# Unit 0 normalised on VectorE and convolved head by head, one Toeplitz side for the first two units, first loads in a new order

## What is computed

```python
x = x + xattn(layernorm(x), k, bias, ctx, ctx, 8)        # v, k, bias, x1, x2
    kv  = v[:, h, i, None, :] * x2[:, h, None, j, :]      # 16 heads of 8 rows
    y   = causal_conv(kv, k[h]) + kv * bias               # 256 positions
    out = sum over i of y[h, i, j, :] * x1[h, i, :]
x = x + ffn(layernorm(x))                                 # 2048 tokens, 16 experts, top 4, and a shared one
```

## Time and profile before

| | |
|---|---|
| time, median of 3 runs | 398.09 us (397.99 to 398.44) |
| span of the profiled execution | 395.4 us |
| mean granted TensorE clock over the span | 0.998 |
| busy: TensorE, VectorE, ScalarE, GpSimd | 384.7, 244.1, 162.9, 180.3 us |

### The profile page before, as it was taken

One profiled execution on the slowest core, in us unless ns is written; L12 is line 12 of the kernel. 1 busy time (PEld: TensorE's weight loads), 2 busy tenths in 40 slices (PEclk: granted clock), 3 DMA queues, 4 the chain that ended last, 5 costly groups with the idle time before them and its releaser, 6 DMA issues.

```text
span 395.4 us, 9070 instructions
## 1 busy us (share of the span) xinstructions
PE 384.7 (97%) x2146; PEld 279.3 (71%) x2147; DVE 244.1 (62%) x676; ACT 162.9 (41%) x494; POOL 180.3 (46%) x225
## 2 busy tenths in 40 slices
PE   6999999999999999999999999999999999999996
PEld 6788888888888546555667675446767777777765
DVE  3577577987988465788735344443445464646466
ACT  5347656564564362101124333333333333334431
POOL 3254323337888573565553333333333333334333
PEclk9999999999999999999999999999999999999999
DMA  7974474368879996256376873334474737362737
GB/s 248 363 254 139 163 277 144 133 206 278 309 250 335 414 419 258 96 207 223 104 215 219 321 239 107 87 95 134 127 246 136 242 115 242 115 232 103 264 97 251
DMA packets 37812, 83.09 MB, mean 210 GB/s; under 512 B 5930, under 2 KB 25870, under 8 KB 35728
## 3 DMA queue, kind: packets, MB, share of 16 engines
q1 hardware_dynamic: 31248, 64.83, 49.1%
q0 software_dynamic: 6528, 17.84, 11.6%
HBM read 60.21 MB, written 23.48 MB: 212 GB/s over the span
## 4 chain that ended last, share of the span: by engine, by line
PE 79%; DVE 10%; DMA 4%; issue 2%; ACT 2%; SPq 1%; DVEq 1%; POOL 0%; POOLq 0%
PE heads L1382 18%; PE bank L1456 13%; PE heads L1271 11%; PE heads L1424 7%; PE heads L1273 5%; PE bank L1437 5%; PE heads L1392 4%; PE bank L1403 4%; PE bank L1285 3%; DVE kv L734 3%; PE heads L1374 3%; DMA toep<-toep_in 2%; PE bank L1448 2%; DVE prod L763 2%; DMA y_scratch<-toep,dest_i 2%
## 5 line engine op out<-in xcount | busy, mean ns | idle before, releaser
L716 POOL DMA_INDIRECT y_scratch<-toep,dest_i x72 | 71.8, 997 | 112.0 <-DVE dest_i L1131 96.0
L1382 PE MATMUL heads<-experts,toep 128*128 x256 | 86.6, 461 | 0.6 <-DVE toep L1089 0.5
L1271 PE MATMUL heads<-toep,kv 128*128 128x256 f32 x256 | 77.9, 386 | 1.9 <-DVE kv L734 0.8
L661 POOL DMA_INDIRECT rows_scratch<-rows,slot_i x64 | 63.3, 989 | 35.4 <-issue 19.5
L1456 PE MATMUL bank<-experts,toep 88*128 x256 | 66.2, 381 | 1.6 <-DVE toep L1096 1.6
L553 ACT ACTIVATE toep<-heads 128x176 f32<-128x176 f32 x72 | 22.8, 317 | 78.1 <-PE heads L1382 67.2
L1382 PEld LDWEIGHTS heads<-experts,toep 128*128 128x128 f32 x256 | 43.7, 190 | 14.8 <-issue 1.1
L1273 PEld LDWEIGHTS heads<-toep,kv 128*128 128x128 f32 x256 | 48.7, 190 | 6.5
L763 DVE TENSOR_TENSOR prod<-heads,ctx_rep 128x1024 f32<-128x1024 f32 x32 | 39.1, 1221 | 22.3 <-PE bank L1285 19.9
L1096 DVE COPY toep<-heads 88x256 f32<-88x256 f32 x72 | 30.2, 419 | 31.1 <-PE heads L1392 31.1
L1273 PE MATMUL heads<-toep,kv 128*128 128x128 f32 x256 | 49.2, 274 | 0.0
(11 more groups left out here) (240 smaller groups left out, 513.4 us busy)
## 6 DMA issues: line engine op xcount, KB each, us to landing
ctx_rep<-ctxr_in SPq DMA_DIRECT2D x16, 1024.0 KB, 5.0
experts<-experts_in SPq DMA_DIRECT2D x16, 608.0 KB
toep<-rows_scratch SPq DMA_DIRECT2D x56, 144.0 KB
prod<-y_scratch SPq DMA_DIRECT2D x5, 1024.0 KB, 5.5
rows_scratch<-pad_row SPq DMA_DIRECT2D x17, 144.0 KB, 1.8
ctx_tr<-ctxt_in SPq DMA_DIRECT2D x16, 128.0 KB
toep<-toep_in SPq DMA_DIRECT2D x4, 512.0 KB, 7.0
ctx_n<-ctx_in SPq DMA_DIRECT2D x16, 128.0 KB, 2.1
```

What stands on the lines that cost most here:

```text
L661: pool.indirect_dma_start(rows_d, bass.IndirectOffsetOnAxis(ap=slot_i[:, u, k:k + 1].bitcast(U32), axis=0), rows[:, u, :], None).then_inc( ...
L716: pool.indirect_dma_start(y_d, bass.IndirectOffsetOnAxis(ap=dest_i[b][:, 0:1].bitcast(U32), axis=0), y_sb[b], None, bounds_check=TOPK * TO ...
L1271: nc.tensor.matmul(y_ps[par][:, i, :], kv[:, q, 0, h * P:(h + 1) * P], toep[:, q * HH + h, :], start=True, stop=False)
L1382: last = nc.tensor.matmul(up_ps[p], x_tr[p][:, blk, :], up_w(e, blk), start=blk == 0, stop=blk == LB - 1)
```

## The change

Units 1 and 2 change places in the processing order (`ORDER`), so that the first two units both hold heads 0 to 7; `SIDE` tells each place's half of `toep` and of `skip_w`. The second Toeplitz half is loaded behind unit 1's context and unit 2's ctx_tr, and `convolve` waits for it at u = 2. Within `toep` and `ctx_rep` heads are stored even first, then odd; a half of `toep` is waited for by parity, and ctx_rep of units 0 and 1 comes in two transfers, one for each parity. x of unit 0 has a transfer and a semaphore of its own.

Unit 0 is normalised on VectorE (`first_v`, with the power still on GpSimd); ScalarE starts with unit 1. The even heads' outer product of unit 0 is made and signalled head by head (`kv_heads_even`), and `convolve(0, 0)` waits for each head. In unit 0 VectorE does `kv_blocks(1)` before both products, and TensorE does `skip_sum(0)` after `convolve(0, 1)`. `skip_w` is made on GpSimd, behind the bias, which is loaded later. There are 14 and 4 warm-up transposes instead of 22 and 10. The host permutes the inputs and puts the output back in order.

```diff
+ORDER = (0, 2, 1) + tuple(range(3, UNITS))
+SIDE = tuple(u % 2 for u in ORDER)
...
-WARM_UP = 22
-WARM_ON = 10
+WARM_UP = 14
+WARM_ON = 4
...
+            def load_rep_half(u, par):
+
+                half = HH // 2 * L
+                sp.dma_start(ctx_rep[:, u, par * HH // 2:(par + 1) * HH // 2, :].rearrange("p h l -> p (h l)"),
+                             ctxr_d[u][:, par * half:(par + 1) * half]).then_inc((rep_odd if par else cr_in)[u], 16)
...
-            load_x(0, 2, x_in[0])
+            load_x(0, 1, x_first)
+            load_x(1, 2, x_in[0])
+            load_tr(0)
+            load_toep(0, 0)
+            load_toep(0, 1)
+            load_tr(1)
+            load_rep_half(0, 0)
+            load_n(0)
             sp.dma_start(bias_c[:], bias_d).then_inc(bias_in, 16)
-            load_tr(0)
-            load_toep(0)
-            load_n(0)
-            load_rep(0)
-            load_tr(1)
+            load_rep_half(0, 1)
             load_x(2, 4, x_in[1])
-            load_toep(1)
             load_n(1)
-            load_rep(1)
+            load_rep_half(1, 0)
+            load_rep_half(1, 1)
+            load_tr(2)
+            load_toep(1, 0)
+            load_toep(1, 1)
             sp.dma_start(wg[:], wg_d).then_inc(wg_in, 16)
...
-            for u in range(2):
-                moments1(u)
-                shift1(u)
-                norm1(u)
+            moments1(1)
+            shift1(1)
+            norm1(1)
...
-            rstd1(0)
+            pool.wait_ge(stat0, 3)
+            nc.gpsimd.tensor_tensor(ln1[:, 0, 3:4], ln1[:, 0, 2:3], neg_half[:], ALU.pow).then_inc(first_rstd, 1)
             rstd1(1)
+            pool.wait_ge(bias_in, 16)
+            for i in range(2):
+                nc.gpsimd.tensor_scalar(skip_w[:, i, :], blocks[:], bias_c[:, i:i + 1], None, ALU.mult
+                                        ).then_inc(skipw_ready, 1)
             v_ctx(0)
...
+            def first_v():
+
+                dve.wait_ge(x_first, 16)
+                nc.vector.bn_stats(stats0[:, 0:6], resid[:, 0, :]).then_inc(stat0, 1)
+                dve.wait_ge(stat0, 1)
+                nc.vector.bn_aggr(ln1[:, 0, 0:2], stats0[:, 0:6]).then_inc(stat0, 1)
+                dve.wait_ge(stat0, 2)
+                nc.vector.tensor_scalar(ln1[:, 0, 2:3], ln1[:, 0, 1:2], EPS, None, ALU.add).then_inc(stat0, 1)
+                dve.wait_ge(first_rstd, 1)
+                nc.vector.tensor_scalar(v_forward(0), resid[:, 0, :].rearrange("p (b n) -> p b n", b=LB), ln1[:, 0, 0:1],
+                                        ln1[:, 0, 3:4], ALU.subtract, ALU.mult).then_inc(v_ready, 1)
+
+            def kv_heads_even():
+
+                dve.wait_ge(ctr_in[0], 16)
+                dve.wait_ge(vt_ps, 1)
+                for h in range(0, HH, 2):
+                    for blk in range(LB):
+                        last = nc.vector.tensor_tensor(
...
+                    last.then_inc(kv_even, 1)
...
-            kv_half(0)
-            kv_half(1)
-
+            first_v()
+            kv_heads_even()
+            kv_heads_odd()
...
+                if u == 0:
+                    kv_blocks(1)
+                    product(0, 0)
+                    product(0, 1)
+                    skip_term(0)
+                    continue
                 product(u, 0)
...
+                if u in (0, 2):
+                    pe.wait_ge(toep_in[u + par], 16)
+                if u >= 1 or par == 1:
+                    pe.wait_ge(kv_ready, u + 1)
                 if u >= 1:
                     pe.wait_ge(prod_ready, 2 * u - 1 + par)
                 for i in range(HH // 2):
                     h = par + 2 * i
...
+                    shifts = toep[:, SIDE[u] * HH + par * HH // 2 + i, :]
+                    if u == 0 and par == 0:
+                        pe.wait_ge(kv_even, i + 1)
...
-                skip_sum(u)
+                if u >= 1:
+                    skip_sum(u)
                 if u + 1 < UNITS:
                     transpose_v(u + 1)
                 if u >= 2:
                     transpose_xn(u - 2)
                 convolve(u, 1)
+                if u == 0:
+                    skip_sum(0)
```

More of the change, by code:

```diff
@@ L204, in build @@
         x_in = [sem(f"x_in{n}") for n in range(5)]
+        x_first, stat0, first_rstd = sem("x_first"), sem("stat0"), sem("first_rstd")
+        rep_odd = [sem(f"rep_odd{q}") for q in range(2)]
         ctr_in, cn_in, cr_in = ([sem(f"{n}{q}") for q in range(2)] for n in ("ctx_tr_in", "ctx_n_in", "ctx_rep_in"))
@@ L747, in kv_half @@
                         last = nc.vector.tensor_tensor(
-                            kv[:, 0, blk, :].rearrange("p (h m i j) -> p h m i j", m=2, i=C, j=C)[:, par::2, m],
-                            tr_ps[:, blk, :].rearrange("p (h m i) -> p h m i", m=2, i=C)[:, par::2, m].unsqueeze(3)
+                            kv[:, 0, blk, :].rearrange("p (h m i j) -> p h m i j", m=2, i=C, j=C)[:, 1::2, m],
+                            tr_ps[:, blk, :].rearrange("p (h m i) -> p h m i", m=2, i=C)[:, 1::2, m].unsqueeze(3)
                             .to_broadcast([P, HH // 2, C, C]),
-                            ctx_tr[:, 0, blk, :].rearrange("p (h m j) -> p h m j", m=2, j=C)[:, par::2, m].unsqueeze(2)
+                            ctx_tr[:, 0, blk, :].rearrange("p (h m j) -> p h m j", m=2, j=C)[:, 1::2, m].unsqueeze(2)
                             .to_broadcast([P, HH // 2, C, C]), ALU.mult)
-                last.then_inc(kv_ready if par else kv_even, 1)
+                last.then_inc(kv_ready, 1)
             def product(u, par):
@@ L1270, in convolve @@
                     h = par + 2 * i
-                    nc.tensor.matmul(y_ps[par][:, i, :], kv[:, q, 0, h * P:(h + 1) * P], toep[:, q * HH + h, :],
-                                     start=True, stop=False)
-                    last = nc.tensor.matmul(y_ps[par][:, i, P:], kv[:, q, 1, h * P:(h + 1) * P],
-                                            toep[:, q * HH + h, 0:P], start=False, stop=True)
+                    shifts = toep[:, SIDE[u] * HH + par * HH // 2 + i, :]
+                    if u == 0 and par == 0:
+                        pe.wait_ge(kv_even, i + 1)
+                    nc.tensor.matmul(y_ps[par][:, i, :], kv[:, q, 0, h * P:(h + 1) * P], shifts, start=True, stop=False)
+                    last = nc.tensor.matmul(y_ps[par][:, i, P:], kv[:, q, 1, h * P:(h + 1) * P], shifts[:, 0:P],
+                                            start=False, stop=True)
                 last.then_inc(conv_done, 1)
@@ L1295, in skip_sum @@
                     pe.wait_ge(skip_ready, u)
-                nc.tensor.matmul(g_ps, skip_w[:, u % 2, :], vc[:, u % 2, :], start=True, stop=True).then_inc(g_done, 1)
+                nc.tensor.matmul(g_ps, skip_w[:, SIDE[u], :], vc[:, u % 2, :], start=True, stop=True).then_inc(g_done, 1)
             def transpose_xn(u):
@@ L1533, in tiles, with by_parity @@
         a = np.asarray(a).reshape(B // 2, 2, 2, HH, C, L).transpose(0, 2, 3, 1, 4, 5)
-        return a.reshape(UNITS, P, L)
+        return a.reshape(UNITS, P, L)[list(ORDER)]
+    def by_parity(a, axis):
+        return np.concatenate([np.take(a, range(par, HH, 2), axis=axis) for par in range(2)], axis=axis)
     ctx_u = tiles(ctx_2048)
@@ L1561 @@
     got = run_bass_kernel_spmd(nc, [arrays], core_ids=[0]).results[0]["out"]
-    got = np.asarray(got).reshape(B // 2, 2, HH, 2, C, L).transpose(0, 3, 1, 2, 4, 5)
+    got = np.asarray(got)[np.argsort(ORDER)].reshape(B // 2, 2, HH, 2, C, L).transpose(0, 3, 1, 2, 4, 5)
     return np.ascontiguousarray(got.reshape(B, D, L))
```

67 lines of the change are left out of this document (29 added, 38 removed).

## The result

| | before | after |
|---|---|---|
| time, median of the runs made side by side | 397.97 us (397.29 to 398.44) | 394.72 us (393.91 to 397.25) |
| span of the profiled execution | 395.4 us | 393.2 us |

The ratio is 0.9925, interval 0.9905 to 0.9945: 3.25 us or 0.75% faster, 2.2 to 3.8 us by the interval. Repeats of the unchanged pair on other occasions gave 0.993 and 0.9938.

A forecast was written before the change was run, and what follows sets the result against it. TensorE was taken to bound the kernel, so the end moves with unit 1's first convolution: 15.50 - 14.35 = 1.15 us off the 395.4 span gives 394.25; with 2.7 us to the median, forecast 396.9 us, range 395.9 to 399.0.

The forecast's parts named there:

- what bounds the kernel: Whole kernel: TensorE holds 79% of the chain that ended last, almost all of it from the second unit on.
- the way to price the change: Start: forecast the new time of unit 1's first convolution, 15.50 to 14.35 us; the end moves with it.
- the relay: Start of unit 0: x lands, normalise, transpose, outer product, then first convolution; 2.2 us gained, 0.9 hidden behind the Toeplitz load.
- the landing of the first Toeplitz part: Load queue at the start: left at 7.5 us, bounds 7.1 and 7.9, so the first convolution starts at 7.65.
- the relay is the bound: Rival at the start: Toeplitz part lands by 6.6, first convolution at 6.75, time 396.0 us; chance 0.10.
- The relay's parts: Unit 0: normalising on VectorE sums to 2.26 us instead of 3.20; outer product pieces 0.20 us apart, first head at 6.63.
- VectorE's order: Unit 0: unit 1's outer product before the even product makes the pair end 6.62 instead of 6.32 us after first convolution's start.
- the cover of 0.9 us: Unit 0: skip_w to 11.5, vc to 12.3, skip matmul asks at 13.2 us, so moving skip_w to GpSimd costs nothing.
- gain taken back: Rival: late bias or new load order holds unit 1's convolution, needing 1.15 us beyond covers; 398.1 us, chance 0.13.
- The clock rival: Rival: TensorE's clock falls in the idle time before the first convolution, costing 1.45 to 2.6 us; 398.5 us, chance 0.27.
- The forecast's gap of 1.3 us: Before the first convolution: TensorE idle until 7.65 us, between idle stretches where the clock level held and where it fell.
- The 2.7 us: Whole kernel: difference between the profiled span of 395.4 and the median of 398.09 us, taken to stay after the change.

## Why the prediction was right or wrong

**Right: what bounds the kernel, and the way to price the change.** The moment of unit 1's first convolution carried most of the gain (1.85 of 2.90 us), unit 2's stays 7.4 behind it, and the relation between the first convolution and unit 1's held: 14.35 - 7.65 = 6.70 forecast, 6.78 in the traces where nothing else holds it. It is right too that the first convolution is released by its Toeplitz load and no longer by the relay: in the four traces of the changed kernel it starts within 0.05 us of that load's landing (6.62, 6.51, 6.48, 6.54), while the first head's outer product had been done at 6.25, 6.31, 6.00 and 6.23.

**The step that failed: the landing of the first Toeplitz part.** The forecast kept it at 7.5 (7.1 to 7.9), because the same 384 KB stand ahead of it in the same issue slot. It landed at 6.5 to 6.6. The two things changed in its front, the bias's rows and x in two transfers, were weighed by their bytes; the run with the old front, and all traces sorted by their front, show that they held this load back by about 0.7 us (which of the two was not tried apart). The mechanism was right and this term was a microsecond too large.

**The rival "the relay is the bound", given 0.10, came near in its numbers and not in its mechanism.** Its condition, a landing by 6.6, came true, and its 6.75 for the first convolution stands against 6.53 to 6.66, its 2.05 us off unit 1's against 2.19 where the bias is early. But the relay had its first head ready by 6.0 to 6.3, not 6.63, and the load still came last. That the two numbers agree is luck.

**The relay's parts were sized well.** The statistics took 0.43 (0.42 taken), the aggregate 0.18 (0.18), the normalisation 0.41 (0.42), the eight pieces of 128 columns are 0.20 apart ((1.67 - 0.28) / 7, 0.20 taken). x landed by 2.90 where 3.35 was taken, and the relay is early by about that.

**VectorE's order does not give 0.3 back.** The even product was taken to be free to start first; ctx_rep would have held it until 10.1. The step compared the two orders by VectorE's durations and left out the load that the earlier convolution now meets.

**`skip_w` was mis-sized.** Its two scalings take 0.60 each, not "no more than 0.40": the row they were sized by is that of another operation. The bias lands at 9.9 to 11.6 in the four traces, where 10.7 was taken, and the skip matmul can run a microsecond sooner than the forecast's 13.2, because the first convolution does. So the cover of 0.9 us is gone, and exceeded by 0.1 and 0.8 in two of the four traces. The rival "gain taken back" had this mechanism, but not the 1.15 us that it needed.

**The clock rival is real, but not this kernel's usual case.** In the changed kernel the first convolution finds the higher level, or reaches it by the second head (at 7.3, 6.4 and 4.8 us in three traces; the first of them lost 0.3 us by it). The forecast's gap of 1.3 us became at most 0.69 with the earlier landing; behind 0.95 and 1.08 in other runs the heads ran at the higher level, behind 1.87 the level fell and the whole gain went. Of another way to the same loss the forecast says nothing: with the old front and without the transposes the level did not fall, it had not yet risen (11.0 and 11.5). From the first convolution to unit 1's these three runs take 8.31, 8.50 and 9.18 instead of 6.78: 1.5, 1.7 and 2.4 us, within the 1.45 to 2.6 that the rival was priced at.

**Missing altogether: the end.** The forecast held that everything behind unit 1 just moves along, and put the end at nothing. From the last matmul's start on it got 0.6 us shorter, since the number of ScalarE's instructions changed and a code packet fell elsewhere, as far as one trace of each variant shows. No step of the working counted instructions of an engine off the path. The start alone, with 1.85 us, would have stayed inside the range, which ends 2.2 us below the time before; start and end together, 2.4, leave it.

**Span and time.** The 2.7 us between the span of 395.4 and the median 398.09 joined one execution's span to other executions' median; where a run has both for the same execution 1.7 to 1.8 us lie between (2.3 in a single one). The profiled execution was a quick one. The difference forecast does not hang on it.

**Open.** About 0.5 us between unit 1's first convolution and the last matmul, as much as single traces scatter; what the later landing of the old front costs in time; and how often the clock rises too late.

## What to carry to other kernels

Before a load is taken as the next bound, ask what stands ahead of it in the queue by transfers, and not by bytes alone: behind a 1 KB transfer of tiny rows and an undivided one this load landed about 0.7 us later. A part can pay only beside another (the signal by head needs a load that is there in time), and one that looks needed may not be (the exchange of units), so price the parts together and try each by taking it out. When a rival's number comes true, check its mechanism before crediting it: here the load was still last. Where two kernels differ by half a microsecond at a place whose code is the same, look for code packets.

## What the hardware showed that was not expected

A code packet of 8 KB inside the last store of a kernel went with an end 0.6 us later (4.04 against 3.45 after the last matmul's start); eight satisfied waits on ScalarE moved it out, eight on SyncE did not. The granted clock fell to 0.50 in the middle of unbroken work, 1.3 us after TensorE had resumed from 1.87 us of standing still, and stayed there 3.4 us. With the changed kernel's transposes ahead, the higher level came at 4.8 us in one execution and at 7.3 in another of the same kernel, and at 11.0 in one with the old front. With no transposes of the identity ahead, the first convolution ran at the lower level for 4.9 us of work (6.57 to 11.5).
